# Two cross-attention blocks on one core: where the softmax sums are inverted, how keys are staged, and how the start and the fills are ordered

## The reference

```python
def _attn(x, ctx, wq, wk, wv, wo, bo, heads):
    q, k, v = heads_of(x @ wq), heads_of(ctx @ wk), heads_of(ctx @ wv)
    a = softmax(einsum('bhid,bhjd->bhij', q, k) * dh ** -0.5)
    out = einsum('bhij,bhjd->bhid', a, v)
    return merge(out) @ wo + bo
for l in range(2):
    h1 = _ln(x, n1_g, n1_b); x = _attn(h1, h1, q1, k1, v1, o1_w, o1_b, 20) + x
    h2 = _ln(x, n2_g, n2_b); x = _attn(h2, context, q2, k2, v2, o2_w, o2_b, 20) + x
    h3 = _ln(x, n3_g, n3_b); a, g = split(h3 @ ff_w1 + ff_b1)
    x = (a * gelu(g)) @ ff_w2 + ff_b2 + x
```

## Time and profile before

| | |
|---|---|
| median of three runs | 3956.21 us |
| profiled execution | 3958.47 us, span 3956.7 us |
| PE busy | 3320.3 us (84%), 16320 matmuls |
| DVE busy | 1963.4 us (50%) |
| ACT busy | 2025.5 us (51%) |
| POOL busy | 671.3 us (17%) |
| DMA queue of SP | 366.50 MB, 30.3% of 16 engines |
| mean granted PE clock | 0.898 |

### The profile page before, as it was taken

How to read it: one execution, slowest core, us unless ns; L and a number is a source line. 1 busy time by engine, 2 the same in 40 slices (tenths; PEclk the granted TensorE clock), 3 DMA queues, 4 the chain that set the end, 5 groups by cost and what they waited for, 6 DMA issues and landing times.

```text
span 3956.7 us, 44936 instructions
## 1 busy us (share of the span) xinstructions
PE 3320.3 (84%) x16320; PEld 1522.7 (38%) x16320; DVE 1963.4 (50%) x2449; ACT 2025.5 (51%) x3936; POOL 671.3 (17%) x710
## 2 busy tenths in 40 slices
PE   1478788899789897899789987898988998999967
PEld 0223233334335343454335442353434543454434
DVE  0245355555555564555555564455645565456500
ACT  0254356555555565655555554545655455546621
POOL 3121202220220204010220213202031004001010
PEclk7688888889899998999889997899979999999979
DMA  8342233422232314322332334333133303312202
GB/s 119 119 128 73 89 103 109 133 80 84 90 116 88 112 51 127 97 93 81 96 127 86 108 106 128 122 99 104 39 102 101 106 31 121 102 35 74 70 18 67
DMA packets 217116, 369.37 MB, mean 93 GB/s; under 512 B 35576, under 2 KB 117888, under 8 KB 215616
## 3 DMA queue, kind: packets, MB, share of 16 engines
q1 hardware_dynamic: 216896, 366.50, 30.3%
HBM read 234.42 MB, written 120.82 MB: 90 GB/s over the span
## 4 chain that ended last, share of the span: by engine, by line
PE 60%; SPq 10%; DVE 9%; DMA 8%; ACT 6%; POOL 4%; issue 3%; ACTq 0%; DVEq 0%; POOLq 0%
PE pr L1013 13%; PE po L1028 12%; PE pd L994 6%; DVE mx L833 6%; PE pf L946 5%; PE pf L954 5%; PE pf L893 4%; PE pf L934 3%; DMA cT<-OU 3%; PE pf L925 2%; PE pf L916 2%; ACT ET L764 2%; SPq L543 2%; SPq L476 2%; SPq L591 2%
## 5 line engine op out<-in xcount | busy, mean ns | idle before, releaser
L833 DVE TENSOR_REDUCE mx<-pd 128x2 f32<-128x804 f32 (+2 forms) x1600 | 1597.1, 1035 | 1237.1 <-PE pd L994 1232.2
L764 ACT ACTIVATE ET<-pr 128x512 f32<-128x512 f32 (+1 forms) x2720 | 1478.3, 597 | 857.8 <-PE pr L1013 847.1
L1013 PE MATMUL pr<-QS,KS 64*128 64x512 f32 (+1 forms) x2720 | 937.8, 519 | 94.3 <-ACT ET L764 89.8
L994 PE MATMUL pd<-KS,QS 64*128 64x400 f32 (+2 forms) x3200 | 685.4, 394 | 198.7 <-DVE mx L833 100.3
L1028 PE MATMUL po<-ET,V 128*32 128x512 f32 (+2 forms) x5440 | 786.1, 653 | 30.6 <-ACT OU L770 29.3
L1013 PEld LDWEIGHTS pr<-QS,KS 64*128 64x128 f32 (+1 forms) x2720 | 366.5, 190 | 1012.0 <-ACT ET L764 655.5
L994 PEld LDWEIGHTS pd<-KS,QS 64*128 64x128 f32 x3200 | 386.1, 198 | 297.9 <-DVE mx L833 155.4
L677 POOL TENSOR_TENSOR OU<-OU,SH 128x512 f32<-128x512 f32 x80 | 101.5, 1269 | 1652.8 <-DMA SH<-inverses 1652.8
L662 POOL TENSOR_TENSOR HS<-uT,HS 128x512 fp32r<-128x512 f32 (+2 forms) x168 | 190.3, 1135 | 707.3 <-ACT uT L732 707.2
L729 ACT ACTIVATE HS<-pf 128x512 fp32r<-128x512 f32 (+2 forms) x168 | 91.2, 543 | 409.6 <-PE pf L893 200.5
L946 PE MATMUL pf<-HS,WS 128*128 128x512 f32 x800 | 239.0, 430 | 42.3 <-DVE uT L826 22.4
(11 more groups left out here) (63 smaller groups left out, 2181.3 us busy)
## 6 DMA issues: line engine op xcount, KB each, us to landing
KS<-scr_k SPq DMA_DIRECT2D x80, 801.0 KB, 6.2
WS<-parts SPq DMA_DIRECT2D x160, 320.0 KB, 2.9
QS<-scr_q SPq DMA_DIRECT2D x160, 256.0 KB, 6.0
scr_k<-HS SPq DMA_DIRECT2D x144, 200.0 KB
scr_q<-HS SPq DMA_DIRECT2D x96, 256.0 KB
KS<-scr_k SPq DMA_DIRECT2D x80, 256.0 KB, 3.6
scr_k<-HS SPq DMA_DIRECT2D x48, 256.0 KB
SH<-inverses SPq DMA_DIRECT2D x320, 32.0 KB, 1.8
```

The lines of the kernel that those rows point to most:

```text
L764: activation(ET[0:q.rows[k], s % 2, h, :], pr[h % 2][0:q.rows[k], :], ACT.Exp).then_inc(score_free, 1)
L833: v.reduce_max(mx[:, t, 2 * p:2 * p + 2, c], pd[no % 2][:, :, 0:cols], AX_X).then_inc(unit_free, 1)
L994: ins = mm(pd[no % 2][:, e, 0:cols], queries[:, t * P:(t + 1) * P], keys, start=True, stop=True)
L1013: mm(pr[h % 2][0:m, :], keys, queries, start=True, stop=True).then_inc(score_ready, 1)
```

## The change

- The four sum rows are no longer placed, stored and read back. One DMA repeats them 16 times each from `OU` straight to a denominator tile `DEN`, at the same rows where the four row DMAs put the group's rows in `OA` ("slot": two groups, one on each half of the partitions, or the fifth alone). When a slot is complete DVE inverts it in four parts of 128 columns, 13, 15, 17 and 19 beats after the group's end, and POOL divides in place at beat 20. There are 48 slots, so 192 reciprocals instead of 80.
- The constant rows of `KS` are set once by four DVE memsets and the key scratch has only the 48 data rows. A group is staged with three DMAs instead of four, with one semaphore.
- At the start only batch 0 of X, the first weights and one scratch tensor's zeros come ahead of the first stores; context, other batches, weights and three more scratch tensors follow behind the first staging.
- Units end earlier and the turn comes 5 beats after the last unit instead of 3, where there is room.
- On 557 beats (`LATE`) ACT evicts the fill behind the next two exponentials instead of ahead of them. Neighbouring key tiles of the cross values are copied with one instruction. The fills of a phase come in another order.

```diff
     else:
         seq = places("v1", i) if i is not None else places("v2b", c)
-        seq += places("o1", c + 1) + (places("o2", c - 1) if c else [])
-        seq += places("v2b", c) if i is not None else []
-        seq += places("tc", c + 1)
-        seq += mixed(places("k2", c + 1, 0, 6), places("n2", c + 1)) + places("t2", c + 1)
-        seq += mixed(places("q2", c + 1), places("n3", c - 1) if c else []) + places("k2", c + 1, 6)
+        seq += (places("o2", c - 1) if c else []) + places("o1", c + 1)
+        cross = places("tc", c + 1)
+        if i is not None:
+            seq += mixed(places("v2b", c), places("n2", c + 1))
+        else:
...
     _from = max(_at + 5, _free, 0)
-    _to = 4 * _q.step0 - 5
+    _lag = 5 if 4 * _q.step0 - _from >= 24 else 3
+    _to = 4 * _q.step0 - _lag - (4 if _lag == 5 else 2)
     if _q.kind == "S":
         _to = min(_to, _from + 8)
     _beats = [b for b in range(_from, _to) if b % 2 == 0]
     for _b, _n in zip(_beats, shares(len(_q.units), len(_beats))):
         UNITS_AT[_b] += _n
-    TURN_AT[_beats[-1] + 3] = _q
-    _free = _beats[-1] + 4
+    TURN_AT[_beats[-1] + _lag] = _q
+    _free = _beats[-1] + _lag + 1
...
-AFTER = {"copy": 5, "place": 5, "invert": 8, "store": 9, "spread": 11, "divide": 14, "move": 16}
+COPY, MOVE, INVERT, DIVIDE = 5, 6, (13, 15, 17, 19), 20
...
+def ended_slot(beat, behind):
+    q = ended(beat, behind)
+    return q if q and (q.g % 2 or q.g == G - 1) else None
...
+LATE = {b for b in PLACES if 0 <= b < BEATS and b % 4 == 1 and fills_at(b) < 2 and not fills_at(b + 2)}
+def repeated(a, rows, row, times):
+    (pitch, partitions), free = a.ap[0], list(a.ap[1:])
+    return bass.AP(a.tensor, a.offset + row * pitch, [[rows * pitch, partitions // rows], [0, times]] + free)
...
-                for p in range(2):
-                    h = q.g * HG + 2 * p
-                    sp.dma_start(KS[:, p, q.at:q.at + q.keys].bitcast(F32),
-                                 ks[h:h + 2].rearrange("e r n -> (e r) n")).then_inc(staged[q.ring][p], 16)
-                    sp.dma_start(QS[:, q.ring, p, :].bitcast(F32),
-                                 qs[h:h + 2].rearrange("e r n -> (e r) n")).then_inc(staged[q.ring][p], 16)
-            def place_sums(q):
+                if q.g == 0 and q.i < 2:
+                    sp.wait_ge(scratch_set[kinds[0], q.i], 16)
+                qs, ks = qs[q.g * HG:q.g * HG + HG], ks[q.g * HG:q.g * HG + HG]
+                for e in range(2):
+                    sp.dma_start(KS[ROWS * e + ROWS - DATA:ROWS * e + ROWS, :, q.at:q.at + q.keys].bitcast(F32),
+                                 ks.rearrange("(p e) r n -> r e p n", e=2)[:, e]).then_inc(staged[q.ring], 16)
+                sp.dma_start(QS[:, q.ring, :, :].bitcast(F32), qs.rearrange("(p e) r n -> (e r) p n", e=2)
+                             ).then_inc(staged[q.ring], 16)
+            def move_rows(q):
                 sp.wait_ge(sums_out, q.n + 1)
-                if q.n:
-                    sp.wait_ge(inverse_stored, 16 * q.n)
+                if q.i:
+                    sp.wait_ge(fill_ready, filled("o1" if q.kind == "S" else "o2", q.i - 1))
...
+                if slots_before(q):
+                    sp.wait_ge(divided[q.kind], slots_before(q))
+                to = slice(64 * (q.g % 2), 64 * (q.g % 2) + 64)
                 for h in range(HG):
-                    row = 32 * h + DH
-                    sp.dma_start(SUMS[8 * h:8 * h + 8, 0, :],
-                                 OU[row:row + 1, q.n % 2, :].rearrange("o (a n) -> o a n", a=8)
-                                 ).then_inc(sums_placed, 16)
-            def store_inverses(q):
-                sp.wait_ge(inverted, q.n + 1)
-                if q.n:
-                    sp.wait_ge(inverse_spread, 16 * HG * q.n)
-                sp.dma_start(inverses.rearrange("h (a n) -> (h a) n", n=64), SUMS[:, 1, :]).then_inc(inverse_stored, 16)
-            def spread_inverses(q):
-                sp.wait_ge(inverse_stored, 16 * (q.n + 1))
-                if q.n:
-                    sp.wait_ge(divided, q.n)
-                for h in range(HG):
-                    sp.dma_start(SH[32 * h:32 * h + DH, :], inverses[h:h + 1, :].partition_broadcast(DH)
-                                 ).then_inc(inverse_spread, 16)
-            def move_rows(q):
-                sp.wait_ge(divided, q.n + 1)
-                if q.i:
-                    sp.wait_ge(fill_ready, filled("o1" if q.kind == "S" else "o2", q.i - 1))
-                for h in range(HG):
-                    to = 64 * (q.g % 2) + DH * h
-                    sp.dma_start(OA[q.kind][to:to + DH, q.g // 2, :], OU[32 * h:32 * h + DH, q.n % 2, :]
-                                 ).then_inc(moved, 16)
-            for b in range(B):
-                sp.dma_start(X[:, b, :, :], x[b].rearrange("(t p) d -> p t d", p=P)).then_inc(x_in, 16)
-                if b == 0:
-                    for which, what, l in LOAD_BEHIND[None]:
-                        if which in ("a", "b"):
-                            load_weights(which, what, l)
-                    for l in range(L):
-                        sp.dma_start(gcol[:, l, :, :, :], w["gains"][l]).then_inc(small_in, 16)
-                        sp.dma_start(b1col[:, l, :, :], w["ff_b1"][l]).then_inc(small_in, 16)
-            sp.wait_ge(consts, CONSTS)
+                    sp.dma_start(OA[q.kind][to.start + DH * h:to.start + DH * h + DH, q.g // 2, :],
+                                 OU[32 * h:32 * h + DH, :]).then_inc(moved, 16)
+                sp.dma_start(DEN[q.kind][to, :], repeated(OU[:, :], 2 * DH, DH, DH)).then_inc(moved, 16)
+            def set_scratch(k, i):
+                sp.dma_start(scr[k, i][:, 0:ROWS - DATA, :].rearrange("h r n -> r h n"),
+                             DEN["C"][0:ROWS - DATA, :].rearrange("p (o n) -> p o n", o=1).to_broadcast([ROWS - DATA, H, T])
+                             ).then_inc(scratch_set[k, i], 16)
+            def load_x(b, own):
+                sp.dma_start(X[:, b, :, :], x[b].rearrange("(t p) d -> p t d", p=P)).then_inc(own, 16)
+            load_x(0, x_first)
...
-            for p in range(2):
-                for k in ("q", "k"):
-                    for which in ("1", "2"):
-                        to = scr[k + which, p]
-                        n = to.shape[2]
-                        ones = ET[0:2, :, :, :].rearrange("p (o a) h n -> p o (a h n)", o=1)
-                        zeros = ET[32:32 + DH, :, :, :].rearrange("p (o a) h n -> p o (a h n)", o=1)
-                        for r, src, rows in ((MAX_ROW, zeros, DH),) if k == "q" else (
-                                (MAX_ROW, ones, 2), (MAX_ROW + 2, zeros, DH - 2)):
-                            sp.dma_start(to[:, r:r + rows, :].rearrange("h r n -> r h n"),
-                                         src[0:rows, :, 0:n].to_broadcast([rows, H, n])).then_inc(scratch_set[p], 16)
-            for which, what, l in LOAD_BEHIND[None]:
-                if which not in ("a", "b"):
-                    load_weights(which, what, l)
-            load_context(0)
+            set_scratch("q1", 0)
...
+                if beat == FIRST_BEAT:
+                    load_context(0)
+                    load_x(1, x_in)
+                    for which, what, l in LOAD_BEHIND[None]:
+                        if which not in ("a", "b"):
+                            load_weights(which, what, l)
+                    set_scratch("q1", 1)
+                    for b in range(2, B):
+                        load_x(b, x_in)
+                    set_scratch("q2", 0)
+                    set_scratch("q2", 1)
+                if ended(beat, MOVE):
+                    move_rows(ended(beat, MOVE))
...
-                pool.wait_ge(inverse_spread, 16 * HG * (q.n + 1))
-                gp.tensor_tensor(OU[:, q.n % 2, :], OU[:, q.n % 2, :], SH[:, :], ALU.mult).then_inc(divided, 1)
+                pool.wait_ge(inverted, len(INVERT) * (slots_inverted(q) + 1))
+                rows = OA[q.kind][0:64 * (q.g % 2) + 64, q.g // 2, :]
+                gp.tensor_tensor(rows, rows, DEN[q.kind][0:64 * (q.g % 2) + 64, :], ALU.mult).then_inc(divided[q.kind], 1)
...
-                    for k in range(k0, k1):
-                        m, from_ = KEY_ROWS["C"][k], (k - k0) * heads * DH
-                        ins = copy(V["C"][0:m, k * VROW:(k + 1) * VROW].rearrange("p (h d) -> p h d", d=DH + 1)[:, h0:h1, 0:DH],
-                                   pf[0:m, from_:from_ + heads * DH].rearrange("p (h d) -> p h d", d=DH))
+                    for m, tiles in itertools.groupby(range(k0, k1), key=lambda k: KEY_ROWS["C"][k]):
+                        tiles = list(tiles)
+                        k, n = tiles[0], len(tiles)
+                        to = V["C"][0:m, k * VROW:(k + n) * VROW].rearrange("p (k h d) -> p k h d", k=n, d=DH + 1)
+                        from_ = pf[0:m, (k - k0) * heads * DH:(k - k0 + n) * heads * DH]
```

(89 more changed lines are left out.)

111 lines of the change are left out of this document (52 added, 59 removed).

## The result

The changed kernel takes 3862.66 us (median of four runs, 3857.31 to 3871.23) against 3956.61 in the same session: ratio 0.9767, 95% interval 0.9743 to 0.9791. The forecast was 3740. The direction was right and the gain is 94 us instead of 216, less than half. The profiled execution has a span of 3855.5 us, 101.2 less than the one before.

A forecast was written before the change was run, and what follows sets the result against it. PE was taken as the bound; start 47, steady part 127, clock 30, before 400 us 8 and end 4 sum to 216 us off the profiled 3958.47, hence 3740 as median; own range 3695 to 3800, 8 in 10 within 3655 to 3885.

The forecast's parts named there:

- The start, 47 us: Up to the first score: less waiting for SP's queue, less the memsets and late batches of X; 47 us won.
- 8 before 400: The 220 us before 400 us, gaining at the same rate as the steady part; 8 us won.
- The wait for the maxima, 75 us: Steady part, 400 to 3800 us: PE's wait for split maxima falls from 88.0 to about 13 us; 75 won.
- Unit buffers, 13 us: Steady part: PE's wait for unit buffers DVE has not reduced falls from 87.7 to 75 us; 13 won.
- Exponentials, 29 us: Steady part: with exponentials ahead of the fill, PE's wait for them falls from 84.0 to 55 us; 29 won.
- copy of `po`: Steady part: the copy comes before the fill, so PE's wait falls from 29.3 to 10 us; 19 won.
- rival (c): Slower: `pf` comes free later on 557 beats, late fills hold up PE; 4020 us at 0.5 us each; chance 0.05.
- Reciprocals, 34 us: Steady part: 192 reciprocals of 934 ns add 135 us on DVE, of which a quarter reaches PE; 34 us lost.
- Staged queries: 70.2 to 45, 25: Steady part: with fewer DMAs in SP's queue, PE's wait for staged queries falls from 70.2 to 45 us; 25 won.
- The clock, 30 us: 400 to 3800 us: a dozen fewer stalls mean less PE time at the lower clock level; 30 us won.
- The end, 4 us: After the last group: PE's wait falls from 15.0 to 10.9 us; 4 us won.
- Rival (a): Only the start pays: all added reciprocal time reaches PE and the clock does not recover; 3880 us, chance 0.18.

The follow-up runs named there:

- f2: The changed kernel with units spread as before and the turn 3 beats after the last unit instead of 5; 3880.09 us, ratio 0.9805 to the kernel before.
- e4: The changed kernel with `LATE` empty, so ACT evicts every fill ahead of the exponentials as before; 3882.95 us, ratio 0.9817 to the kernel before.
- f3: The changed kernel inverting only 8 of each 128 columns of the denominators; 3829.36 us, ratio 0.9685 to the kernel before.
- e5: The changed kernel with all staging as before: 128-partition key loads, keys and queries by head pair, a semaphore each; 3770.89 us, ratio 0.9528 to the kernel before.
- g1: The changed kernel with old staging, no memsets, last phase's fills in old order, plus units 9 beats after staging instead of 5; 3805.60 us.
- e2: The changed kernel with key loads filling all 128 partitions, still three DMAs and one semaphore a group; 3803.26 us, ratio 0.9620 to the kernel before.

## Why the prediction was wrong, by its own steps

- **The start, 47 us, and 8 before 400: right.** 58.5 were won. The memsets' 7.8 us by the reductions' rate is 7.85 from start to start (the row itself says 6.25, with 1.6 of idle ahead of it), and the four take 31.3 us, from the end of the cast at 8.82 to the statistics at 40.14. The first score is 3 us later than said, PE's wait for X 9 us instead of 12. The Trainium skill's cycle per element (VectorE: DVE Perf Modes, section "Zero memsets can be issued as uint32 (trn2)"), an estimate of 7.7 us at that page's 0.96 GHz, agrees with the trace; the cast's rate does not.
- **The wait for the maxima, 75 us: right,** with about 37 of it the turn's (f2) and the rest the sums'. DVE's wait in front of the reciprocal fell only from 163.0 to 91.4 us, so "next to no wait for DMA" was wrong. Nor is it harmless where two reciprocals stand in front of DVE's copy of the turned maxima, as at 1008.92 above.
- **Unit buffers, 13 us: near, but partly by luck.** 40 went, although the units are denser, and 29 came back in front of units as the wait for DVE's copies (12.4 to 41.0), which the prediction did not have. **Exponentials, 29 us: too large,** 84.0 to 74.5. With the copy of `po` (29 went, 19 said) the two terms together were 48 and the rows give 39, from which the late fills' 34 us of waits for eviction go off again. The prediction put these at nothing outside rival (c), though "if PE waits for evicted fills" was among its signs of being wrong. By e4 the late fills as a whole are worth 20.
- **Reciprocals, 34 us: right** (922 ns each, 934 said; 33 us in f3's median, 15 in its profile).
- **"Staged queries: 70.2 to 45, 25" is the step that failed.** It went to 181.7. The prediction laid the wait at 1526 us on SP's queue and counted DMAs. It said that "part of that is the load itself", and that part is most of it: the last 5.6 of the 8.30 us. It put the smaller key loads at nothing because DMA has idle time, and the runs show them landing after 10.3 us instead of 6.2. It named that "PE now waits for all of it" and gave it no price. Yet the load must run between the end of one group and the first unit of another, 5 beats later, so there its duration is on the path, whatever the mean share of the engines. Undone, it gives 139 us of the long stretch, more than the 119 that it fell short by.
- **The clock, 30 us: not seen,** mostly for the same step. 0.92 stayed where over 0.94 was expected, and PE is busy 86%, not 91%. Of PE's idle times those over 3 us add up to 241 us in 300 to 3700, and to 184 before: there is more of it, at other places. With staging undone (e5) the granted clock is 0.94 in 400 to 3600 us.
- **The end, 4 us: right in size, partly by luck.** 4.3 were won, 2.7 of them at the wait of the earlier trace rows. The landing of the last DMA was put at 1.5 us, for which no row stood, and the reciprocals begin 3.9 us behind the end of its issue; from the copy to the first fill it is 12.4 us instead of the 10.9 worked out.

With staging as before (e5) the long stretch wins 177 us against the 157 of the forecast, although staged queries still cost 90.4. The mechanism of the rest stood in the main, with its terms off in both directions; they were not parted to the end. One edit, booked at a gain, cost most of it. None of the rivals was this one. Rival (a) gives nearly the measured time, 3880. It was right that the clock does not recover, but its mechanism, all the reciprocals' time reaching PE, is refuted by f3 and PE's unit waits. That DVE has idle time to spare holds only as long as units are spread: in g1 it became the wait at once.

What stays open: why such a load runs at half the rate. That it does is shown by e2 against the changed kernel, but e2 changes two things at once: a narrow load has 48 rows instead of 128, and all of them lie on one half of the partitions (16 to 63 or 80 to 127). A load of as few rows spread over both halves would part them and was not tried. Nor was it tried to issue the two halves from two queues at once, or, with narrow loads, to issue the cross group's behind the self group's.

## What to carry to other kernels

A load that is issued when a buffer comes free and wanted a few microseconds later can be on the path, as here, so price its landing time and what the first consumer waits for, not its bytes or the mean share of the DMA engines. Give the first consumer a semaphore for just the part that it reads. When a change cuts the number of DMAs, look at what shape the remaining ones have: "fewer and smaller" was here slower and later.

## What the runs showed of the hardware

- With key rows of 6.4 KB going into 48 partitions on one half, the DMA engines, all busy, move 190 GB/s, and about 400 with rows going into 128 partitions (the windows at 1435 and 1526 us). Leaving a quarter of the bytes out of a cross group's keys made their landing 4 us later (801.0 KB in 6.2 us, 600.8 KB in 10.3); a self group's, in rows of 2 KB, land after 3.6 us in both kernels (256.0 and 192.0 KB).
- A DVE memset of 7432 fp32 columns takes 7.85 us from start to start, on 2 partitions as on 16, and its row shows 6.25 of it, with the missing 1.5 to 1.6 us as idle time ahead of the row: behind the last one the next instruction starts at once.
